# A latent attention layer of a fused decoder: the order of the work that fills its pipeline

## The reference, cut to what matters

```python
x = x + L0_attn(layernorm(x)) ; x = x + L0_xattn(layernorm(x), ctx) ; x = x + L0_ffn(layernorm(x))

# L1_attn: N_HEADS = 8, HEAD_DIM = 64, KV_LRANK = 64
q = (x @ Wq.T).reshape(b, t, N_HEADS, HEAD_DIM)
kv_latent = x @ Wkv_down.T
k = (kv_latent @ Wk_up.T).reshape(b, t, N_HEADS, HEAD_DIM)
v = (kv_latent @ Wv_up.T).reshape(b, t, N_HEADS, HEAD_DIM)
attn = softmax(einsum('bqhd,bkhd->bhqk', q, k) * HEAD_DIM ** (-0.5))
out = einsum('bhqk,bkhd->bqhd', attn, v).reshape(b, t, N_HEADS * HEAD_DIM) @ Wo.T

# L1_xattn: one head of 256 over the context
q = Q @ Wq + bq ; k = K @ Wk + bk ; v = V @ Wv + bv
scores = where(mask == 0, -1e9, einsum('bqd,bkd->bqk', q, k) * scale)
out = einsum('bqk,bkd->bqd', softmax(scores), v) @ Wo + bo

x = x + L1_ffn(layernorm(x))
```

## Time and profile before

| | |
|---|---|
| Median of 3 runs | 1688.71 us (1688.21 to 1689.14) |
| The profiled execution's own time | 1701.78 us |
| Its span | 1700.1 us |
| TensorE busy | 1529.8 us, 90% of the span |
| VectorE, ScalarE, GpSimd busy | 979.5, 848.2, 482.1 us |
| Mean granted clock of TensorE | 0.963 of full speed |

### The profile page before, as it was taken

One profiled execution on the slowest core, in us unless ns is written; L12 is line 12 of the kernel. 1 busy time (PEld: TensorE's weight loads), 2 busy tenths in 40 slices (PEclk: granted clock), 3 DMA queues, 4 the chain that ended last, 5 costly groups with the idle time before them and its releaser, 6 DMA issues. The chain is left out here.

```text
span 1700.1 us, 26952 instructions
## 1 busy us (share of the span) xinstructions
PE 1529.8 (90%) x10059; PEld 1067.3 (63%) x10059; DVE 979.5 (58%) x2273; ACT 848.2 (50%) x1849; POOL 482.1 (28%) x584
## 2 busy tenths in 40 slices
PE   6999999998978879999999899999999979995199
PEld 4677766766755668877877466665666634442088
DVE  3665776766757335222222566767665555599883
ACT  4455565645555422221122556666656533597980
POOL 3222224243234320000001665455532300163000
PEclk9999999998999989999999999999999979997599
DMA  3440111111151143344344211111100000000032
GB/s 114 154 153 17 46 30 43 33 42 42 34 163 38 49 151 112 111 149 130 111 129 128 83 38 51 32 38 32 38 13 13 1 25 1 0 0 20 18 92 69
DMA packets 100928, 108.30 MB, mean 64 GB/s; under 512 B 25410, under 2 KB 89804, under 8 KB 100800
## 3 DMA queue, kind: packets, MB, share of 16 engines
q1 hardware_dynamic: 94656, 90.01, 17.0%
q0 software_dynamic: 6144, 16.57, 3.1%
HBM read 64.77 MB, written 42.01 MB: 63 GB/s over the span
## 5 line engine op out<-in xcount | busy, mean ns | idle before, releaser
L1780 POOL TENSOR_SCALAR c_pr<-c_pr,c_rsum 128x256 f32<-128x256 f32 x256 | 128.5, 518 | 185.7 <-DVE c_rsum L2193 184.9
L2071 ACT ACTIVATE c_pr<-bank,c_nmax 128x256 f32<-128x256 f32 x256 | 118.0, 474 | 118.1 <-DVE c_nmax L2188 110.6
L1511 ACT ACTIVATE b_G<-bank 128x320 f32<-128x320 f32 x128 | 56.0, 438 | 209.9 <-PE bank L1461 209.9
L1461 PE MATMUL bank<-b_XT,shared 128*128 128x320 f32 x512 | 153.7, 435 | 0.0
L2188 DVE TENSOR_REDUCE c_nmax<-bank 128x2 f32<-128x512 f32 x128 | 82.4, 686 | 105.0 <-PE bank L1839 103.8
L1475 PE MATMUL bank<-shared,b_G 128*128 128x256 f32 x640 | 142.2, 379 | 0.0
L1475 PEld LDWEIGHTS bank<-shared,b_G 128*128 128x128 f32 x640 | 120.9, 190 | 17.8
L492 POOL TENSOR_TENSOR a_L<-a_L,a_Lm 128x1232 f32<-128x1232 f32 x32 | 72.0, 2249 | 164.7 <-DVE a_Lm L1075 164.7
L1060 DVE TENSOR_TENSOR hT_all<-bank,a_causal 128x512 f32<-128x512 f32 x128 | 79.4, 683 | 65.6 <-PE bank L557 65.6
L1461 PEld LDWEIGHTS bank<-b_XT,shared 128*128 128x128 f32 x512 | 92.0, 192 | 27.2 <-issue 0.6
L1530 DVE COPY b_Y<-bank 128x256 f32<-128x256 f32 x80 | 34.0, 425 | 120.3 <-PE bank L1475 120.1
(11 more groups left out here) (365 smaller groups left out, 3409.5 us busy)
## 6 DMA issues: line engine op xcount, KB each, us to landing
shared<-L_ffn_w SPq DMA_DIRECT2D x32, 512.0 KB, 6.1
t_slots_in<-a_h SPq DMA_DIRECT2D x20, 512.0 KB, 7.2
shared<-t_slots_in SPq DMA_DIRECT2D x15, 640.0 KB, 7.1
t_slots_out<-b_Y SPq DMA_DIRECT2D x15, 640.0 KB, 4.1
hT_all<-x SPq DMA_DIRECT2D x8, 512.0 KB, 4.0
a_xr<-x SPq DMA_DIRECT2D x8, 512.0 KB, 3.8
t_x_a<-a_x SPq DMA_DIRECT2D x8, 512.0 KB, 2.8
shared<-t_x_a SPq DMA_DIRECT2D x8, 512.0 KB
```

What stands on the lines that cost most here:

```text
L1461: t = p.matmul(P[2 + n % 2][:, 0:HC], w1[e % 3][:, u, 128 * f:128 * f + 128], XT[e % 2][:, u, HC * m:HC * m + HC], start=(u == 0), stop=(u ...
L1780: p.tensor_scalar(pr[k][:, e, u, :], pr[k][:, e, u, :], rsum[k][:, e, u:u + 1], 1.0, ALU.mult, ALU.mult).then_inc(q.pr_ready, 1)
L2071: a.activation(pr[t % 2][:, e, u, :], P[e][:, S * u:S * u + S], ACT.Exp, bias=nmax[t % 2][:, e, u:u + 1], accum_out=sums[t % 2][:, e, u:u ...
```

## The change

It moves five things and changes no arithmetic and no count of operations.

- **The context products.** TensorE no longer makes scores and outputs of both k ahead of everything. It makes those of k = 0, then the turn of the first normalised input (`turn_norm(0, 0)`), then the scores of k = 1 (`late_scores(1)`), and the outputs of k = 1 (`late_outputs(1)`) only in slot 0, after the first `scores`. `scores(0)` now waits for banks 0 and 1 alone, and a new wait ahead of `turn(0)` is for banks 2 and 3.
- **ScalarE** keeps the scores row of k = 0, then both halves of the turned input, then the row of k = 1.
- **VectorE** keeps the outputs of k = 0 where it kept both, and those of k = 1 at the end of slot 0, ahead of the maxima of slot 1.
- **The queries.** Sets 1, 2 and 3 of group 0 are made in slots 0, 1 and 2 (before: 1 and 2 in slot 0, 3 in slot 1). ScalarE keeps sets 2 and 3 in slots 1 and 2 (before: 0 and 1).
- **The second turn.** `turn_norm(0, 1)` and its two copies move from slot 1 to the end of slot 2, and VectorE's `normalise(0, 1, x3[1])` from the front of slot 1, ahead of `by_key(0)`, to its end, behind `invert(1)`.

```diff
 (TensorE)
-                for k in range(NG - NEARLY):
+                def late_scores(k):
                     p.wait_ge(q.l_kept, 2 * k + 2)
                     context_scores(p, P[2 * k], xwqT, bq, kbT[k]).then_inc(q.l_made, 1)
+                def late_outputs(k):
                     context_outputs(p, P[2 * k + 1], xwo, vbT[k]).then_inc(q.l_made, 1)
...
                 def scores(t):
                     if t == 0:
-                        p.wait_ge(q.l_kept, 3 * (NG - NEARLY))
-                        p.wait_ge(q.l_out_kept, NG - NEARLY)
+                        p.wait_ge(q.l_kept, 2 * (NG - NEARLY) + 1)
+                        p.wait_ge(q.l_out_kept, 1)
...
                 def turn(t):
+                    if t == 0:
+                        p.wait_ge(q.l_kept, 3 * (NG - NEARLY))
+                        p.wait_ge(q.l_out_kept, NG - NEARLY)
...
+                late_scores(0)
+                late_outputs(0)
                 p.wait_ge(q.absorb_kept, 8)
                 turn_norm(0, 0)
+                late_scores(1)
                 latent(0)
                 queries(0, 0)
                 latent_keys(0)
...
                     scores(t)
+                    if t < 3:
+                        queries(0, t + 1)
                     if t == 0:
-                        queries(0, 1)
-                        queries(0, 2)
+                        late_outputs(1)
                     if t >= 1:
                         turn(t - 1)
                     if t >= 2:
                         values(t - 2)
...
-                    if t == 1:
-                        queries(0, 3)
...
-                    if s == 1 and ahead:
+                    if s == 1 + (g == 0) and ahead:
                         turn_norm(0, g + 1)
 (ScalarE)
-                for k in range(NG - NEARLY):
+                def keep_scores_row(k):
                     a.wait_ge(q.l_made, 2 * (NG - NEARLY) + 2 * k + 1)
                     a.activation(later.scores_row[NEARLY + k], P[2 * k][:, 0:3 * KX], ACT.Copy).then_inc(q.l_kept, 1)
...
+                keep_scores_row(0)
                 keep_norm(0, 0, [hT0[:, u, :] for u in range(2)])
+                keep_scores_row(1)
...
-                    if t in (0, 1):
-                        keep_unit(f"q{t + 2}", 0, qT[0][:, t + 2, :], bank(f"q{t + 2}", 0)[:, :])
+                    if t in (1, 2):
+                        keep_unit(f"q{t + 1}", 0, qT[0][:, t + 1, :], bank(f"q{t + 1}", 0)[:, :])
...
-                    if s == 1 and ahead:
+                    if s == 1 and behind and ahead:
                         keep_norm(0, g + 1, [hT0[:, u, :] for u in range(2)])
...
                     if t >= 1:
                         by_key(t - 1)
+                    if t == 2:
+                        keep_norm(0, 1, [hT0[:, u, :] for u in range(2)])
 (VectorE)
-                late_context()
+                late_context(0)
...
-                    if t == 1:
-                        normalise(0, 1, x3[1])
                     if t >= 1:
                         by_key(t - 1)
                     invert(t)
                     if t == 0:
                         tile_moments(1, NT - 1)
                         variances(1)
+                        late_context(1)
+                    if t == 1:
+                        normalise(0, 1, x3[1])
```

10 lines of the change are left out of this document (5 added, 5 removed).

## The result

| | before | changed |
|---|---|---|
| median of 16 runs each, us | 1688.77 (1686.14 to 1690.84) | 1691.77 (1689.41 to 1694.49) |
| changed / before, 95% interval | | 1.0018 (1.0011 to 1.0025) |
| profiled execution, us | 1701.78 | 1694.27 |
| its span, us | 1700.1 | 1692.5 |
| mean granted TensorE clock | 0.963 | 0.961 |

The changed kernel is **3.0 us slower** by the medians, where 0.5 us faster was forecast; that lies outside the range. The profiled executions say the opposite, 7.5 us faster. Both are true readings.

The account below looks back on a forecast made before the run. GpSimd was taken as pace maker in slots 0 to 2, TensorE behind them. -1.60 us on TensorE, 1.05 returning as waits, left -0.55: 1688.71 - 0.55 = 1688.2 us, range 1686.1 to 1689.8.

Parts of the forecast that it names:

- clock paragraph: Possible clock fall in the hole from 940.93 to about 943.2 ahead of the first turn: 1.7 us, taken as nothing.
- step 1: First turn ahead of the context scores of k = 1: latent and scores(0) 1.60 us earlier on TensorE.
- slower rival: Clock falls in the new holes (940.9 to 943.2, or 959.2 to 960.4): +0.6 us, 1689.3; chance 0.10.
- second hole: TensorE without work from 959.2 to 960.4, ahead of scores(2); a clock fall behind it would leave 1.2 us.
- deciding point: A clock fall later than 953, when TensorE's slack of 1.6 us is gone, makes the slower rival decide.
- Step 2: maxima(0) still waits for group 1's gathered rows and stays at 952.79: 0 of the 1.60 us arrives.
- all of TensorE's gain arrives: Rival: gathered rows land earlier, so maxima(0) follows scores(0): -2.1 us, 1686.6; chance 0.10.
- Step 3: Query set 1 alone in front: VectorE's copy follows the maxima without waiting, invert(0) and first scaling 0.52 us earlier.
- Steps 4 and 5: Context addition ahead of maxima(1), scores(2) after 1.2 us without work, nobody else waits; group 1's normalising and turn free.
- Step 6: GpSimd's scalings keep their distances, 10.18 us from first to third; from there every start 0.5 to 0.6 earlier.
- The sum: -1.60 us on TensorE ahead of slot 0, of which 1.05 us return as new waits: -0.55 us.
- a stretch that differs by over 1 us: Sign of a wrong forecast: scores(4) to the stage's end differs in length by over 1 us.

Follow-up runs that it names:

- before, third: The kernel before, unedited, measured a third time on an occasion near 1705 us: 1705.42 us, ratio 0.9998.
- order part: The kernel before with only the queries spread over slots 0 to 2 and the second turn a slot later: 1688.45 us (0.9996), 1705.6 us (1.0005).
- Filled twice: The changed kernel plus two unread passes of context column products ahead of the first turn: 1701.88 us (0.9983), 1704.28 us (0.9988), 1691.25 us (1.0008).

## Why the prediction was wrong

**Its clock paragraph and step 1 failed.** The prediction had found the risk and priced it at nothing, after the row at 937.36, where a wait of 2.13 us did not lower the clock. It took one undisturbed hole for a rule, and measured it is 2.37 us of the fill. The row itself did not bear the weight: at the same place in the same kernel a wait of 2.11 us did lower the clock (before, third). Holes of 3.62 and 1.90 us ahead of the turn let it fall too, one of 2.65 us did not. The hole itself was given as 2.3 us (940.93 to 943.2); where ScalarE makes no pauses it is 3.62, since the outputs of k = 0 end at 13.23 from the stage's start and not at 15.57. The Trainium skill's warning on idle TensorE between bursts (TensorE: Matmul & The Clock Gate, section "HAM oscillation — how this bites in real kernels") was cited against step 1 and set aside. The first profile bears it out, with 0.50 at the turn; the holes of 2.13 and 2.65 us that cost nothing do not.

**The price of the slower rival was too small: +0.6 us in all, where the fill lost 2.8.** For the hole ahead of the turn it let 1.7 us of the fall vanish behind the gathered rows, where the fall cost 2.37; its 1.2 us stood for the second hole, behind which the clock did not fall. It set the deciding point at 953, 27.6 from the stage's start. The rows landed at 23.97 instead of 25.52, and the fall itself held the latent, its copy and scores(0). Nothing hid it: scores(0) came 2.8 us later than in the kernel before on an occasion of 1688 us (26.62 against 23.79), and so did scores(4).

**What was saved was not there to save.** The earlier trace rows was read as the kernel; it was the kernel on an occasion on which ScalarE rests between its context copies. On an occasion of 1688.5 us the turn was at 17.43, not 19.8, without the change, and the median of 1688.7 that the forecast started from is of that kind. The 13 us between that execution and the median were noted and passed over with "the difference applies to both". That sentence had no ground.

- *Step 1, on an occasion of 1705 us*, was right to 0.3 us: turn 16.82, latent 19.94, scores(0) 24.31, where 16.7, 20.1 and 24.5 were predicted.
- *Step 2 (0 of the gain arrives, because of the gathered rows)* was wrong there. The gather of the third tile was late in that one execution: 25.52, while it was 23.4 to 24.0 in the other profiles that wait for it. maxima(0) followed at 25.90, and scores(4) came 1.9 us earlier: it followed scores(0) at 20.85, so the rows were not what it waited for. The ground of the step, that no edit comes near the transfer, was wrong as well (the issue of 1.65 us), but that cost nothing here. In the fill that is the rival "all of TensorE's gain arrives" (-2.1). In the time it is not: 1.0002 (0.9989 to 1.0015) and 0.9992 (0.9977 to 1.0006).
- *Step 3 (0.52)*: the order part alone gained 0.13 us in the fill. Its first scaling is at 29.09 against 29.12. In the kernel before on this kind of occasion VectorE waits only 0.16 us for query set 1, not 0.52.
- *Steps 4 and 5* hold in that nobody else waits: scores(2) waits 0.64 us at 952.79 where 1.2 was expected, and the second turn runs at 958.01 without a wait.
- *Step 6* holds: 10.09 us from the first to the third scaling, where 10.18 was taken.
- *The sum* had no term for what follows scores(4). It named a stretch that differs by over 1 us as a sign against itself, and that sign came: 403.15 to 408.65.

**No edit was better than before on both kinds.** Filled twice was faster on one occasion, 0.9983 (0.9972 to 0.9993), and not on two others, 0.9988 (0.9973 to 1.0002) and 1.0008 (0.9996 to 1.0021). I would keep the kernel before, or its order part, which costs nothing that can be told: 0.9996 (0.9984 to 1.0007) and 1.0005 (0.9990 to 1.0019).

## What to carry to other kernels

Before moving filler work out of a wait, ask what the engine does in the hole: context products that look like an obstacle ahead of the turn were what kept TensorE's clock up, and a hole cost 2.4 us in a pipeline's fill. Where a profiled execution lies 13 us from its own median, take a wait that the sum rests on for a property of that execution until a second profile shows it again. And where a change makes a stage's fill shorter, compare the rest of the stage too: here it was up to 5 us longer, for a reason that stays open.

## What was not expected of the hardware

- **The length of a hole alone does not tell whether the clock falls.** 1.90 us: 0.85 and 0.69 behind it. 3.62 us: 0.50. But 2.65 us (ahead of 941.25) and 2.13 us: 1.00. What stood before these differs, but it does not decide either: behind the same instructions of the same kernel 2.13 us left it at 1.00 and 2.11 us brought it down to 0.52 (942.12). What does decide stays open.
- **An issue of a gather on GpSimd can take 1.65 us instead of 1.0 to 1.2**, in all 14 profiles in which VectorE mixes rows beside it, and the third tile's rows land 0.48 us later. No run varied that by itself.
- **Rests of ScalarE of 1.3 to 3.6 us, two or three times between four short copies**, in all 13 profiles of an execution over 1700 us, and in none of the 7 of 1687 to 1694 us. Eight more instructions ahead of them did not move them. The profile puts most of them down to TensorE's products, which were through. What holds ScalarE there stays open.
- **The same kernel takes 1688 or 1705 us by occasion**, on one chip too. Some 2.4 us of it is the fill, some 10 us have come up by the stage's start (912.9 to 916.9 us against 922.1 to 930.3), and ratios on one kind did not carry over to the other: the changed kernel is 1.0018 on the one and 1.0002 and 0.9992 on the other.
